# Row maxima 30 steps ahead of their exponentials rather than 32, and a side plan laid out anew

## The chip, the cores and the metric

One core of a Trainium2 chip runs the whole kernel. TensorE (PE in the profile) multiplies, VectorE (DVE), ScalarE (ACT) and GpSimd (POOL) work elementwise, SyncE (SP) issues nearly all DMAs. The metric is the device time of one execution in microseconds; lower is better. Three runs of the kernel before gave 1772.64, 1775.31 and 1781.6 us, median 1775.31.

## The reference

Eight batches of 1024 tokens with 128 channels pass two blocks, each a modulated layer norm, an attention, another norm and a feed-forward part. Cut to what matters:

```python
# block 0: one head of width 32, causal; scores of 0 are masked too
h = layernorm(x)*(1+ca)+sa;  x = x + ga * softmax(mask(QK/sqrt(32))) @ (h @ (Wvdown@Wvup))
h = layernorm(x)*(1+cb)+sb;  e = argmax(h@Wg+bg) % 8;  x = x + gb * relu(h@We[e]+be[e]) * p
# block 1: 16 heads of width 8, full attention over 1024 tokens
h = layernorm(x)*(1+ca)+sa;  weight = softmax(q k^T / sqrt(8));  x = x + ga * ((weight@v)@Wout+bout)
h = layernorm(x)*(1+cb)+sb;  x = x + gb * ((h@W1[b]+b1[b])@W2[b]+b2[b])
```

The 16-head attention is the bulk: 8 x 16 x 1024 x 1024 scores, each of which is computed twice, once for the row maximum and once, transposed, for the exponential.

## The kernel before

**The main line.** Two heads make a pair; there are 64 pairs, eight to a batch. A unit is 128 rows of a pair by 512 columns for both heads, 16 units to a pair, so 1024 units of each kind in all. A maxima unit is two bf16 products on PE (line 792) and one DVE reduction of 128x1024 from PSUM (line 1329). An exponential unit is two products (line 802), which subtract the maxima by way of three extra rows of `q_ops`, and one ACT exponential (line 1028). A values unit multiplies the exponentials with v (eight f32 products, four of them at once; lines 818, 828), and after 16 of them ACT copies the sums out (line 1037) and SP stores them with four DMAs (line 1636).

**Steps.** All five engines walk the same loop over a step number h, from -2*LEAD to 1025. In step h PE issues the exponential products of unit h (if h is at least 0), the maxima products of unit h + 2*LEAD (while there are any), then no, one or two values units (`value_table`, a table worked out beforehand), then the side stages that the plan has put into this step. DVE does the reduction of unit h + 2*LEAD and then its part of the side stages; ACT the exponential of unit h and then its part; POOL and SP have side stages alone. Each engine takes its instructions in this order and waits on semaphores. With LEAD = 16 the first 32 steps (-32 to -1) have maxima alone and the last 32 (992 to 1023) have exponentials alone. Three PSUM buffers go round between the units (`unit_table`), so the exponential products of step h wait for the reduction of step h - 2, and the maxima products of step h for the exponential of step h - 1.

**From maxima to exponentials.** After the last reduction of a pair DVE joins the halves (stage `maxima`), one step later POOL splits the result into three bf16 parts (`nm_split`, lines 1477 to 1480), five steps after that PE transposes them (`nm`), ACT copies, and SP writes them to `q_ops` with two DMAs (line 1612). The exponentials of the pair wait for those.

**Side stages.** Everything else is cut into stages: block 0 and the feature part of block 1 for batch b run beside the attention of batch b-1, the output part (`sums`, `numerators`, `wout_mm`, `stats_b`, `apply_b`, `x_wff`, `channels_b`, `ffn`) of batch b beside the attention of b+1 and its end. `front_line`, `half_line`, WEIGHTS_LINE, BACK_LINE and NM_LINE are lists of (gap in steps, stage); `lay_out` walks them and moves a stage on to the next step that is free. A step is free when no other stage fills the one side bank of PSUM in it (modulo 128, since a batch is 128 steps) and the stage's engine, DVE or ACT, has no other side stage there. `make_plan` repeats the result for each batch, 128 steps apart. Stages before step -2*LEAD run ahead of the loop in the order of the list ALONE. `value_table` then spreads the values units: it minimizes a sum of squared loads of the steps, in which SWITCH is the charge for a kind of product that a step has, and LIGHT is the load below which a step counts as equal.

The stages that the prediction speaks of: `hm` (POOL, line 1462) multiplies the features of 128 tokens with the expert masks, which SP has written to DRAM and fetched back (`masks_out`, `masks_load`, line 1596); it needs the `moe` stage of two tiles before to be done. `moe_a` and `moe` (PE) are the expert products of a tile, which read `hm`. `residual` (POOL, lines 1470, 1471) closes block 0. `stats` and `stats_b` are DVE statistics (1087, 1090) followed by small POOL operations (1357 to 1359); `apply` and `apply_b` (POOL, line 1365) normalize; `channels` (PE, line 608) transposes the result, `qk1` makes q and k, and `parts` (POOL, lines 1414 to 1417) splits them into bf16 parts, which SP stores with three DMAs each (line 519) after waiting for the split. `load_operands` (SP, line 526) fetches a later pair's operands with four DMAs; LOAD_BEFORE sets its step.

Of the kernel before, what the change touches and what calls it, by code (L numbers as in the profile page):

```python
# [41 lines left out]
SLOTS = 4  # L42
VW = DH + 1
COLUMN_TILE = 32
LEAD = 16
PAIRS = B * HEADS // 2
PERIOD = T * HEADS // 2
UNITS = 2 * T
# [7 lines left out]
def chunks(i):  # L56

    return [(c, min(BANK, (i + 1) * P - c)) for c in range(0, (i + 1) * P, BANK)]


def blocks(i):

    some = list(range(1 if i == T - 1 else 0, i + 2))
    return [some[c:c + 4] for c in range(0, len(some), 4)]
# [9 lines left out]
def front_line():  # L74

    out = [(0, ("stats", 0, 0, 0)), (1, ("stats", 0, 0, 1)), (1, ("stats", 0, 1, 0)), (1, ("stats", 0, 1, 1)),
           (0, ("apply", 0, 0)), (1, ("apply", 0, 1)), (3, ("channels", 0, 0)), (1, ("g0", 0)), (1, ("channels", 0, 1)),
           (1, ("g0", 1)), (1, ("v0",)), (0, ("later",)), (1, ("gates",))]
    for n in range(T + 3):
        if 2 <= n < T + 2:  # L80
            out += [(1, ("transpose_p", n - 2, c)) for c in range(len(blocks(n - 2)))]
        if 1 <= n < T + 1:
            out += [(1, ("softmax", n - 1))]
        if n >= 3:
            out += [(0, ("times_v", n - 3))] + ([(2, ("up", n // 7))] if n - 3 in (3, T - 1) else [])
        if 1 <= n < T + 1:
            out += [(1, ("exp0", n - 1))] + ([(0, ("sums0", n // 5))] if n in (4, T) else [])
        if n < T:
            out += [(0, ("scores", n, c)) for c in range(len(chunks(n)))]
    return out  # L90


def half_line(half):

    first = 4 * half
    out = [(0, ("stats", 1, half, 0)), (1, ("stats", 1, half, 1)), (2, ("apply", 1, half)), (3, ("channels", 1, half)),
           (2, ("wg", half)), (1, ("top", half, 0)), (1, ("top", half, 1)), (1, ("index", half, 0)), (1, ("index", half, 1)),
           (0, ("gating", half, 0)), (2, ("onehot", half)), (0, ("gating", half, 1)), (2, ("onehotT", half)), (1, ("over_gating", half)),
           (0, ("masks_out", half)), (3, ("masks_load", half)), (6, ("hm", first)), (2, ("hm", first + 1)), (1, ("moe_a", first))]
    for t in range(first, first + 4):  # L100
        out += [(3, ("moe_a", t))] if t > first else []
        out += [(1, ("moe", t))] + ([(1, ("hm", t + 2))] if t < first + 2 else [])
    out += [(1, ("residual", half)), (2, ("stats", 2, half, 0)), (1, ("stats", 2, half, 1)), (1, ("apply", 2, half)), (3, ("channels", 2, half))]
    for w in range(2):
        out += [(2 - w, ("qk1", w, half)), (0, ("parts", w, half))]
    return out + [(1, ("v1", half))]
# [25 lines left out]
ON_DVE = {"stats", "softmax", "up", "wg", "top", "index", "onehot", "over_gating", "wff", "wout_mm", "stats_b", "ffn", "maxima"}  # L132
ON_ACT = {"exp0", "gating"} | {name for name, by in EMPTIED_BY.items() if by == "act"} - {"nm"}

FRONT_FROM, WEIGHTS_FROM, BACK_FROM, LOAD_BEFORE = -200, 90, 132, 11

SWITCH, LIGHT = 0.9, 5.1


def quarters(*stage):  # L140
# [4 lines left out]
def lay_out():  # L145
# [6 lines left out]
    def put(line, b, h):  # L152
        ending = False
        for gap, stage in line:
            fills, part = stage[0] in EMPTIED_BY, stage[0].endswith("_a")
            h, stage = h + (1 if ending else gap), (stage[0], b, *stage[1:])
            on = "dve" if stage[0] in ON_DVE else "act" if stage[0] in ON_ACT else None
            if not ending and (line is not NM_LINE or fills):
                while (fills or part) and h % batch in filled or part and (h + 1) % batch in filled or on and h % batch in busy[on]:
                    h += 1  # L160
            if fills or part:
                filled.add(h % batch)
            if part:
                filled.add((h + 1) % batch)
            if on:
                busy[on].add(h % batch)
            ending = part
            at[stage] = h
        return h

    for pair in range(HEADS // 2):
        put(NM_LINE, pair, UNITS * (pair + 1) - 2 * LEAD)
    put(WEIGHTS_LINE, 0, WEIGHTS_FROM)
    put(BACK_LINE, 0, BACK_FROM)
    put(front_line(), 0, FRONT_FROM)
    for half in range(HALVES):
        put(half_line(half), 0, at["up", 0, half] + 1)
# [28 lines left out]
def make_plan():  # L206
# [4 lines left out]
    for (name, n, *more), at in lay_out().items():  # L211
        pairs = name in [stage[0] for gap, stage in NM_LINE]
        for b in range(B):
            h, stage = at + 2 * b * PERIOD, (name, b * HEADS // 2 + n if pairs else b, *more)
            if stage in first:
                continue
            if h < -2 * LEAD:
                ahead.append((h, stage))
# [86 lines left out]
def unit_table():  # L305

    order = []
    for h in range(-2 * LEAD, PAIRS * UNITS):
        if h >= 0:
            order.append(("exp", h))  # L310
        if h + 2 * LEAD < PAIRS * UNITS:
            order.append(("max", h + 2 * LEAD))
    return order, {unit: at for at, unit in enumerate(order)}
# [32 lines left out]
def build(nc, ctx, x_in, Wq0, Wk0, Wvdown, Wvup, Wg, bg, We, be, c0, wmod0,  # L346
# [187 lines left out]
    def tensor_program():  # L534
# [303 lines left out]
        for bank, u in before_steps.items():  # L838
            if bank:
                pe.wait_ge(S["side_" + u.by], u.emptied)  # L840
        for h in range(-2 * LEAD, PAIRS * UNITS + 2):
            if 0 <= h < PAIRS * UNITS:
# [888 lines left out]
```

## Time and profile before

| | us |
|---|---|
| median of three runs | 1775.31 |
| profiled execution, its own time | 1772.89 |
| its span in the trace | 1771.6 |
| maxima-only steps -32 to -1 | 124.7 to 174.1 |
| one full batch of 128 steps (batches 1 to 5 of the loop) | 205.7 to 205.9 |
| the last reduction of line 1329 starts | 1714.3 |

The page lists the busy time of each engine, the granted clock of PE and the costliest lines; views of the trace give windows, waits and timelines. A number x8 behind a row says how many instructions are merged in it. "SPq" rows are DMA issues; the bracket at a row's end is idle time and what ended it. Step numbers below count within a batch of 128; the batch looked at closely starts at 789.9 us (absolute step 384), its step 19 at 818.0 and its step 48 at 867.5.

### The profile page before, as it was taken

The page shows a single profiled execution, that of the slowest core. Times are in us where ns is not written, and L with a number is a line of the kernel's source. Part 1 is how long each engine was busy: PE and PEld are TensorE (multiplying, and loading weights), DVE is VectorE, ACT ScalarE, POOL GpSimd, SP SyncE. Part 2 cuts the span into 40 slices and gives each one's busy share as a digit, 9 for nine tenths or more (in the row PEclk, how much of TensorE's full clock was granted, in tenths as well). Part 3 has the DMA queues.
Part 4 walks back from the last instruction along what each step waited for, and adds up shares of the span by engine and source line. Part 5 has one row for each costly group of instructions (what it writes and reads, how often), then busy time and mean ns, then how long its engine had stood idle before and what let it go on. Part 6 is the DMA issues. An engine that isn't in the chain of part 4 may idle for free.

```text
span 1771.6 us, 54921 instructions
## 1 busy us (share of the span) xinstructions
PE 1668.0 (94%) x23327; PEld 658.5 (37%) x23337; DVE 1499.3 (85%) x2257; ACT 1378.6 (78%) x1934; POOL 733.7 (41%) x1195
## 2 busy tenths in 40 slices
PE   5777999999999999999999999999999999999998
PEld 3543433334333343334333343333433343222224
DVE  4669888898889988899888988899888998999973
ACT  4443779887798778887798878987788877887885
POOL 2321345526543465434564365434664355112110
PEclk9998999999999999999999999999999999999999
DMA  2131111122210322112210213103211122201111
GB/s 71 50 122 33 39 56 53 33 63 59 84 59 23 91 71 69 35 37 74 83 56 27 73 48 94 49 24 96 63 59 36 38 73 71 70 24 50 35 28 35
DMA packets 97234, 99.96 MB, mean 56 GB/s; under 512 B 11117, under 2 KB 81437, under 8 KB 96989
## 3 DMA queue, kind: packets, MB, share of 16 engines
q1 hardware_dynamic: 96188, 95.66, 18.1%
q8 instruction: 184, 3.01, 0.7%
q10 hardware_dynamic: 800, 0.79, 0.1%
q14 instruction: 62, 0.50, 0.1%
HBM read 61.02 MB, written 34.57 MB: 54 GB/s over the span
## 4 chain that ended last, share of the span: by engine, by line
PE 67%; DVE 15%; ACT 13%; issue 3%; DMA 1%; POOL 1%; ACTq 0%; SPq 0%; DVEq 0%; POOLq 0%
PE pv_psum L818 23%; PE side_psum L551 15%; PE buffer L802 12%; PE buffer L792 10%; DVE row_max L1329 9%; ACT p L1028 7%; PE side_psum L641 2%; PE side_psum L608 2%; PE buffer L551 1%; ACT o_sb L1037 1%; DVE s L1177 1%; ACT s L946 1%; DVE st_f L1087 1%; ACT s L939 1%; ACT hT_b L1017 1%
## 5 line engine op out<-in xcount | busy, mean ns | idle before, releaser
L1329 DVE TENSOR_REDUCE row_max<-buffer 128x2 f32<-128x1024 f32 x1024 | 1235.3, 1219 | 163.6 <-PE buffer L792 151.0
L1028 ACT ACTIVATE p<-buffer 128x1024 f32<-128x1024 f32 x1024 | 1048.2, 1025 | 209.1 <-PE buffer L802 193.3
L818 PE MATMUL pv_psum<-p,v 128*9 128x256 f32 x8192 | 583.8, 381 | 5.8 <-ACT o_sb L1037 5.2
L792 PE MATMUL buffer<-k_ops,q_ops 48*128 48x512 bf16 x2048 | 396.1, 384 | 17.8 <-ACT p L1028 7.7
L802 PE MATMUL buffer<-q_ops,k_ops 51*128 51x512 bf16 x2048 | 400.5, 388 | 6.7 <-DVE row_max L1329 5.2
L818 PEld LDWEIGHTS pv_psum<-p,v 128*9 128x9 f32 x8192 | 149.7, 89 | 316.8 <-issue 234.0
L802 PEld LDWEIGHTS buffer<-q_ops,k_ops 51*128 51x128 bf16 x2048 | 98.1, 92 | 371.7 <-issue 237.2
L1462 POOL TENSOR_TENSOR hm<-masks,hT_f 128x1024 f32<-128x1024 bf16 x56 | 120.4, 2150 | 107.5 <-PE side_psum L551 107.5
L792 PEld LDWEIGHTS buffer<-k_ops,q_ops 48*128 48x128 bf16 x2048 | 99.4, 94 | 116.5 <-ACT p L1028 98.7
L1477 POOL TENSOR_SCALAR nm_parts<-nm 128x16 bf16<-128x16 f32 x64 | 16.3, 255 | 268.2 <-DVE nm L1254 267.8
L551 PE MATMUL side_psum<-we,hm 128*32 128x128 f32 x3648 | 121.1, 274 | 0.0
L1445 POOL TENSOR_SCALAR rest<-s 128x128 f32<-128x128 f32 (+7 forms) x48 | 102.8, 2142 | 4.2
L551 PEld LDWEIGHTS side_psum<-we,hm 128*32 128x32 f32 x3648 | 95.1, 110 | 21.6 <-issue 19.3
L1439 POOL TENSOR_TENSOR s<-s,consts 128x128 f32<-128x128 f32 x60 | 27.8, 463 | 166.8 <-ACT s L939 166.8
L1357 POOL TENSOR_SCALAR sm_f<-mv_f 128x4 f32<-128x4 f32 x32 | 6.3, 198 | 180.6 <-DVE mv_f L1090 180.0
L551 PE MATMUL side_psum<-hT,g 128*32 128x512 f32 (+3 forms) x624 | 66.0, 494 | 4.2 <-ACT s L939 2.5
L641 PE MATMUL side_psum<-consts,s 128*128 128x128 f32 x281 | 50.9, 297 | 6.1 <-DVE xn_f L1192 4.4
L946 ACT ACTIVATE s<-s,nm 128x1024 f32<-128x1024 f32 (+6 forms) x60 | 51.4, 857 | 6.4 <-DVE nm L1177 5.9
L1365 POOL TENSOR_SCALAR xn_f<-x,sm_f 128x128 f32<-128x128 f32 x112 | 54.0, 497 | 3.8 <-POOL sm_f L1359 3.8
L957 ACT COPY p0T<-side_psum 128x512 f32<-128x512 f32 (+3 forms) x84 | 43.6, 519 | 12.7 <-PE side_psum L641 10.9
L1177 DVE CUSTOM_DVE_ANT_0 s<-s,rest 128x128 f32<-128x128 f32 (+7 forms) x60 | 45.5, 759 | 4.5 <-POOL rest L1445 4.1
L939 ACT COPY s<-side_psum 128x512 f32<-128x512 f32 (+3 forms) x78 | 37.4, 479 | 13.3 <-PE side_psum L551 11.6
(296 smaller groups left out, 1654.8 us busy)
## 6 DMA issues: line engine op xcount, KB each, us to landing
masks<-masks_rows SPq DMA_DIRECT2D x16, 1024.0 KB, 6.5
q_ops<-products SPq DMA_DIRECT2D x128, 96.0 KB
k_ops<-products SPq DMA_DIRECT2D x128, 96.0 KB
products<-q_parts SPq DMA_DIRECT2D x16, 384.0 KB, 2.6
products<-k_parts SPq DMA_DIRECT2D x14, 384.0 KB, 2.8
attention<-o_sb SPq DMA_DIRECT2D x248, 18.0 KB
x<-in_L_attn_inputs SPq DMA_DIRECT2D x8, 512.0 KB, 4.3
products<-q_parts SPq DMA_DIRECT2D x16, 256.0 KB, 3.0
```

The costliest lines, as they stand in the source:

```text
L551: m = e.matmul(out[q:q + COLUMN_TILE, :], weight[:, q:q + COLUMN_TILE], moving, start=start, stop=stop)
L641: m = e.transpose(v[:, j * P:(j + 1) * P], s0_of(b, i)[0][:, k * P:(k + 1) * P], ident)
L792: m = e.matmul(buffer[:, hh, :], q_ops[rows_of(hh, K_MAX), slot, of, i * P:(i + 1) * P], k_ops[rows_of(hh, K_MAX), slot, of, halves(half)[ ...
L802: m = e.matmul(buffer[:, hh, :], k_ops[rows_of(hh, K_EXP), slot, of, kb * P:(kb + 1) * P], q_ops[rows_of(hh, K_EXP), slot, of, halves(half ...
L818: m = e.matmul(pv_psum[q:q + VW, half * QUARTER:(half + 1) * QUARTER], v1[b % 2][:, kb, 2 * hp + hh, :], p_sb[n % KEPT][:, hh, part * QUAR ...
L939: e.copy(s[:, P + at:P + at + w], v[:, 0:w]).then_inc(S["side_act"], 1)
L946: e.activation(s[:, start:P + n], s[:, start:P + n], ACT.Exp, scale=-1.0, bias=nm0[:, i:i + 1], accum_out=acc0[:, i:i + 1]).then_inc(S["p0 ...
L1028: e.activation(p_sb[n % KEPT][:, :, :], unit("exp", n)[0][:, :, :], ACT.Exp).then_inc(S["exp_done"], 1)
L1177: e.tensor_tensor_reduce(out=s[:, P:P + n], in0=s[:, P:P + n], in1=rest[:, 0:n], scale=1.0, scalar=-NEG, op0=ALU.add, op1=ALU.min, accum_o ...
L1329: e.tensor_reduce(mx[pair % 2][:, :, i, half], unit("max", n)[0][:, :, :], axis=AX.X, op=ALU.max).then_inc(S["max_done"], 1)
L1445: e.tensor_scalar(rest[:, 0:n], s[:, P:P + n], 0.0, -NEG, ALU.is_equal, ALU.mult).then_inc(S["masked"], 1)
L1462: e.tensor_tensor(hm[t % 2][:, :, :], masks[:, :, cols], hT_f[:, cols].unsqueeze(1).broadcast_to([C, EXPERTS, P]), op=ALU.mult).then_inc(S ...
```

## The change

LEAD becomes 15: maxima stand 30 steps ahead. The pair's `maxima` stage, and with it `nm_split` and `nm`, come two steps later against the exponentials, so `nm` is 8 steps ahead of the pair's first exponential instead of 10. `load_operands` comes two steps later as well. Since these stages hold steps that others must avoid, the plan comes out otherwise, and five numbers in it are changed too. The stages ahead of the loop stay the same.

```diff
-LEAD = 16
+LEAD = 15
-... (3, ("channels", 0, 0)), (1, ("g0", 0)), (1, ("channels", 0, 1)),
-           (1, ("g0", 1)), ...
+... (3, ("channels", 0, 0)), (2, ("g0", 0)), (1, ("channels", 0, 1)),
+           (0, ("g0", 1)), ...
-        out += [(1, ("moe", t))] + ([(1, ("hm", t + 2))] if t < first + 2 else [])
+        out += [(1, ("moe", t))] + ([(0, ("hm", t + 2))] if t < first + 2 else [])
-FRONT_FROM, WEIGHTS_FROM, BACK_FROM, LOAD_BEFORE = -200, 90, 132, 11
+FRONT_FROM, WEIGHTS_FROM, BACK_FROM, LOAD_BEFORE = -201, 90, 132, 11
-SWITCH, LIGHT = 0.9, 5.1
+SWITCH, LIGHT = 1.2, 5.1
```

Followed through `lay_out` and `value_table`, the steps of a full batch are (before -> after):

| stage | step | stage | step |
|---|---|---|---|
| `onehotT`, second half | 11 -> 15 | `stats_b` (0,0), (0,1), (1,0), (1,1) | 27, 28, 29, 33 -> 27, 28, 29, 32 |
| `masks_load`, second half | 15 -> 19 | `stats` of block 1, first half | 30, 31 -> 25, 30 |
| `moe` of tiles 0 to 3 | 8, 13, 18, 25 -> 10, 14, 18, 22 | `apply_b`, `apply` of block 1 | 31, 32 -> 31, 31 |
| `hm` of tiles 4 to 7 | 21, 23, 29, 34 -> 25, 27, 29, 33 | `channels` of block 1, first half | 35 -> 34 |
| `moe_a`/`moe` of tiles 4, 5 | 27/28, 32/33 -> 28/29, 32/33 | `parts` of q, of k, first half | 37, 40 -> 36, 38 |
| `wout_mm` | 23, 26 -> 23, 26 | `nm` of the pair of step 48 | 38 -> 40 |
| `residual`, first half | 26 -> 23 | `load_operands` | 37 -> 39 |
| values units in steps 0-18, 19-47, 48-127 | 18, 30, 80 -> 19, 31, 78 | values copied and stored | 19, 34 -> 19, 35 |

Both plans have values or tile work in 121 of the 128 steps, and the same side stages. SP's order in a step is `load_operands`, the store of the values, then the plan's stages.

## Rows read from the trace of the kernel before

**Rows 1.** The page: busy us, share of the span, instructions of each engine.
```profile
PE 1668.0 (94%) x23327; PEld 658.5 (37%) x23337; DVE 1499.3 (85%) x2257; ACT 1378.6 (78%) x1934; POOL 733.7 (41%) x1195
```

**Rows 2.** Windows: length, busy us of each engine, granted clock, DMA share, GB/s.
```profile
124.70:174.10 49.40, 38.64 (x320) 15.37 (x322) 46.77 (x81) 13.89 (x33) 6.89 (x19) 0.88 0.15 48
...
789.90:818.00 28.10, 27.81 (x466) 12.38 (x466) 26.30 (x40) 22.99 (x33) 12.45 (x16) 1.00 0.34 99
818.00:867.60 49.60, 48.02 (x822) 21.38 (x822) 41.13 (x59) 36.31 (x44) 31.51 (x41) 1.00 0.21 64
867.60:995.80 128.20, 124.16 (x1595) 44.90 (x1593) 112.96 (x170) 111.06 (x163) 58.68 (x104) 1.00 0.16 49
...
1590.40:1714.30 123.90, 119.27 (x1307) 34.41 (x1308) 118.55 (x123) 102.07 (x110) 17.12 (x43) 1.00 0.14 39
1714.30:1752.00 37.70, 36.49 (x582) 15.66 (x586) 8.00 (x14) 32.88 (x37) 3.64 (x6) 1.00 0.11 29
```

**Rows 3.** Timeline of DVE: start, us, line, operation.
```profile
124.69 4.69 DVE L1329 TENSOR_REDUCE row_max<-buffer 128x2 f32<-128x1024 f32 x4 [0.48 <-PE buffer L792]
...
877.08 1.19 DVE L1329 TENSOR_REDUCE row_max<-buffer 128x2 f32<-128x1024 f32 x1
...
878.87 2.33 DVE L1329 TENSOR_REDUCE row_max<-buffer 128x2 f32<-128x1024 f32 x2
```

**Rows 4.** Timeline of PE, steps 24 to 35; each step begins with line 802.
```profile
825.61 0.39 PE L802 MATMUL buffer<-q_ops,k_ops 51*128 51x512 bf16 x2
...
826.59 0.24 PE L551 MATMUL side_psum<-be,onehotT 128*32 128x128 bf16 x4 [0.37 <-DVE x L1303]
...
827.63 0.39 PE L802 MATMUL buffer<-q_ops,k_ops 51*128 51x512 bf16 x2
...
833.17 0.39 PE L802 MATMUL buffer<-q_ops,k_ops 51*128 51x512 bf16 x2
...
835.13 0.39 PE L802 MATMUL buffer<-q_ops,k_ops 51*128 51x512 bf16 x2
...
836.65 0.39 PE L802 MATMUL buffer<-q_ops,k_ops 51*128 51x512 bf16 x2
...
845.66 0.66 PE L608 MATMUL side_psum<-consts,xn_f 128*128 128x128 f32 x4
```

**Rows 5.** Timeline of POOL, from `hm` of tile 5 to the k split.
```profile
829.37 2.15 POOL L1462 TENSOR_TENSOR hm<-masks,hT_f 128x1024 f32<-128x1024 bf16 x1 [8.38 <-PE side_psum L551]
...
839.48 1.75 POOL L1365 TENSOR_SCALAR xn_b<-x,sm_b 128x128 f32<-128x128 f32 x4
...
843.06 1.75 POOL L1365 TENSOR_SCALAR xn_f<-x,sm_f 128x128 f32<-128x128 f32 x4 [0.18 <-POOL sm_f L1359]
...
851.35 2.35 POOL L1528 TENSOR_TENSOR x<-x,wff 128x1024 f32<-128x1024 f32 x1
...
860.12 1.16 POOL L1417 TENSOR_TENSOR k_parts<-xn_f,k_parts 128x512 bf16<-128x512 f32 x1
```

**Rows 6.** Timeline of SP's DMA issues in the same stretch.
```profile
809.87 0.54 SPq L1596 DMA_DIRECT2D masks<-masks_rows  x1
820.18 3.35 SPq L1636 DMA_DIRECT2D attention<-o_sb  x4
...
848.40 1.47 SPq L526 DMA_DIRECT2D q_ops<-products  x2
...
859.14 1.59 SPq L1612 DMA_DIRECT2D q_ops<-nm_rows  x2
861.31 2.03 SPq L519 DMA_DIRECT2D products<-k_parts  x3
```

**Rows 7.** Tile `masks`: issue to landing of its 16 loads.
```profile
DMA to landing us min/median/max: 5.5/6.5/8.3
```

**Rows 8.** DMA issues by line: a short transfer, KB each, us to landing.
```profile
over_sums_rows<-sums SPq DMA_DIRECT2D x7, 64.0 KB, 1.6
```

More of the change, by code:

```diff
@@ L76, in front_line @@
     out = [(0, ("stats", 0, 0, 0)), (1, ("stats", 0, 0, 1)), (1, ("stats", 0, 1, 0)), (1, ("stats", 0, 1, 1)),
-           (0, ("apply", 0, 0)), (1, ("apply", 0, 1)), (3, ("channels", 0, 0)), (1, ("g0", 0)), (1, ("channels", 0, 1)),
-           (1, ("g0", 1)), (1, ("v0",)), (0, ("later",)), (1, ("gates",))]
+           (0, ("apply", 0, 0)), (1, ("apply", 0, 1)), (3, ("channels", 0, 0)), (2, ("g0", 0)), (1, ("channels", 0, 1)),
+           (0, ("g0", 1)), (1, ("v0",)), (0, ("later",)), (1, ("gates",))]
     for n in range(T + 3):
```

## The prediction
> **What bounds the kernel now.** I read the page first: PE is busy 94% of the span, DVE 85% [rows 1]. Then the windows by stage, since the share is an average [rows 2]. In the 32 steps that have maxima alone DVE is busy 46.8 of 49.4 us: DVE bounds them. In the long middle a batch of 128 steps takes 28.1 + 49.6 + 128.2 = 205.9 us, and PE is busy 27.8 + 48.0 + 124.2 = 200.0 of them; the granted clock is 1.00 there, so PE at its full clock bounds the middle, and what isn't PE's own work are short waits. From 1590 to 1714 DVE is busy 118.6 of 123.9 us and bounds again. The last 37.7 us have exponentials alone, and PE is busy 36.5.
>
> The middle's steps have fixed prices, which the timeline of PE shows [rows 4]. A step with two values units and no side stage goes from 835.13 to 836.65, 1.52 us. One with one values unit and the four-tile stage `moe` goes from 833.17 to 835.13, 1.96. A values unit is half of what a pair of them adds, 0.44; so exponential and maxima products with their changeover take 0.64, and a four-tile stage 0.88 to 0.90. A wait shows as a step above its price: the step from 825.61 to 827.63 has `moe_a` alone (0.64 + 0.90 = 1.54) and took 2.02, because `moe_a` right behind `wout_mm` waits for DVE to empty the one side bank (0.37 idle in its row).
>
> By this rule the number of values units, tile stages and changeovers decides PE's own work, and both plans have the same per batch. What the change can move are the ends and the waits.
>
> **The change part by part.**
>
> *The ends.* Two steps with maxima alone go. Four reductions in a row start at 124.69 and take 4.69 us, and two take 2.33 to 2.36 [rows 3], so one is 1.13 to 1.18; DVE bounds this stretch, its other work stays and now lies in 30 steps: -2 x 1.15 = -2.3 us. At the other end steps 992 and 993 get a reduction that they hadn't. A step there costs 37.7 / 32 = 1.18 on average, and one of the DVE-bound stretch before it 123.9 us over 102 steps (890 to 991) = 1.21, so by these averages nothing is lost; but the lightest of the exponential-only steps have less PE work than a reduction takes (0.39 and less of products beside one values unit [rows 4]); I take +0.25 each, +0.5. Ends: -1.8 us.
>
> *Steps 48 to 127 and 0 to 18.* The table puts 78 values units instead of 80 into the first and 19 instead of 18 into the second: -0.88 and +0.44. The chain of side stages keeps its distances, because it slides as a whole by two steps. In 0 to 18, `moe_a` no longer stands right behind `onehotT`, and the two steps of `top` have two values units each in place of one of them having one, so DVE's four long steps there are better covered: I take back 0.5. In 48 to 127 `wff_a` now follows `transpose_p` without a values unit to cover the emptying by ACT, +0.2. Together -0.1 and -0.7 per batch. Seven passes of the first and six of the second, and a seventh without block 0 at -0.3: -0.7 - 4.5 = -5.2 us. Bounds: each of these waits is between nothing and the 0.48 that the `moe_a` step lost above, so 3 us to either side over the run.
>
> *Steps 19 to 47* (49.6 us before, of which PE idles 1.6). Three things come together here, in the six passes that have the output part (the first pass has none and comes out at +0.3).
> First, `masks_load` goes from step 15 to 19, behind the four stores of values on SP. Those were issued from 820.18 to 823.53, the load at 809.87 [rows 6]. Now it is issued at 823.6 (step 19 at 818.0 in both, so clock times compare). Its landing takes 6.5, 5.5 at least and 8.3 at most [rows 7]: 830.1. POOL's `hm` for tile 4 starts then; before, it ran at 818.8.
> Second, POOL's queue behind it. Two `hm` of 2.15 end at 834.4. The small operations of `stats_b` wait for DVE's statistics. DVE's turn is 1.12 for a reduction and 1.79 with statistics beside it (877.08 to 878.87 [rows 3]); for steps 25 to 30 that makes the statistics of step 28 ready at 835.6. Small operations 1.6, `hm` 2.15, small ones 1.8 (between 841.23 and 843.06 [rows 5]), two normalizations of 1.75: 835.6 + 1.6 + 2.15 + 1.8 + 3.5 = 844.6. `channels` of step 34 needs that. PE comes there with 15 steps x 0.64 + 15 values units x 0.44 + 8 four-tile stages x 0.90 + `nm` 0.15 = 23.5, at 841.6 with 0.1 for the clock, and is at the side stage 1.0 later, 842.6 to 842.7. So PE waits 1.9 us. Before, the normalization ended at 844.81 and `channels` ran at 845.66, a step later: no POOL wait.
> Third, SP. From the normalization to the end of the k split POOL took 861.28 - 844.81 = 16.5 us before [rows 5], and the queue is the same but for its order: 861.1 after. SP comes to `parts` of q (step 36) and of k (38) before `load_operands` (39) and `nm` (40). Before, the k split was the last: the maxima rows went out at 859.14, ahead of the k stores at 861.31 [rows 6]. Now they are queued behind the wait for the k split, the three k stores (2.05), four operand loads (1.47 + 1.43), and one output store of 0.5: 861.1 + 5.45 = 866.6. Two issues of 0.8, the second landing 1.6 after it begins: 869.0. I bound this landing by 1.6 (the shortest seen [rows 8]) and 3.0 or more if the 768 KB of k parts lie before it; I take the short one, since the rows are 6 KB. PE reaches step 48 at 842.7 + 1.9 + the rest of step 34 and the 13 steps 35 to 47 (23.8) = 868.4 and waits 0.6.
> So step 48 starts at 869.0 rather than 867.5: +1.5 us, six times +9.0, and the first pass +0.3: +9.3 us. Bounds: if POOL and SP hold nobody up, the stretch costs its own work plus 0.5 of bank waits, 48.2, which is -1.4 x 6 = -8.4; if masks land at 8.3 and the rows take 3.0, it is 1.8 + 1.4 more, less some of the first that is absorbed, +2.5 x 6 = +15 on top.
>
> The Trainium skill bears on the last point (DMA: Bandwidth & Descriptors, "Queues, rings and completion order"): a semaphore's increment lands only after every earlier write of the same DMA engine, so a small transfer signals no sooner than the large ones issued before it. No row here shows the landing of the maxima rows. By that rule the landing would be at the long end, and the slower case below would be the likely one; the sum doesn't use it.
>
> Sum: -1.8 - 5.2 + 9.3 = +2.3 us on the profiled execution's own 1772.9, so 1775.2. The median of the runs shown lies 2.4 above it: 1777.6, rounded to 1778.
>
> **The rivals.**
> *The maxima rows come later still (slower).* In steps 36 to 48 SP is one queue, and the exponentials of the pair of step 48 wait at its end. From the point where the rows land after 868.4 every microsecond is paid six times. With 8.3 for the masks or 3.0 for the rows, about +2.5 a pass on top, +15: 1793. For: the slack was 867.5 - 861.6 = 5.9 us before and I count it as used up; DVE's statistics, which POOL waits for, stand in six of the steps 25 to 32 without the extra values units that covered them. Against: waits on PE give POOL and SP their time back. Chance 0.24.
> *The chain doesn't bind (faster).* If `hm` of tile 4 starts early enough, or PE arrives at 34 later than I count because DVE's statistics hold it anyway, one wait takes the other's place, and the removed bank waits (0.48 behind `wout_mm`, 0.4 in front of `qk1`) count: 9.3 - (-8.4) = 17.7 less, 1760. For: `residual` and `moe` of tile 3 come three steps earlier, POOL idled 8.38 us before `hm` at 829.37 [rows 5] and has this time to give. Against: that idle time is where the masks are now awaited. Chance 0.21.
> *It does nothing in the middle.* Waits exchanged one for one, only the ends count: 1773.5. It lies inside my forecast's range; chance 0.10.
> My forecast as it stands: 0.45.
>
> **How the numbers follow.** Within 0.5% is about what a measurement of this kernel can tell from no change: 1766.4 to 1784.2. The forecast's own range is 1769 to 1785. It and the third rival put 0.50 inside and leave 0.03 and 0.02 on the slower and faster side. The slower rival reaches from 1783 to 1796 and is 0.23 outside, the faster one from 1758 to 1767 with 0.20 outside. Faster 0.22, same 0.52, slower 0.26. For 8 in 10 the range takes in half of each rival: 1762 to 1790.
>
> **What would show it.** The maxima-only stretch at 47.1 us instead of 49.4. In each of six passes `channels` behind a POOL wait of 1 to 2 us at step 34; SP issuing the maxima rows of the pair of step 48 behind the k stores; `masks` loads of the second half after the four stores. A batch at 205.9 + 1.5 - 0.8 = 206.6 us; 209 would mean the slower rival, 204 the faster. I am wrong in the mechanism if PE's waits in steps 19 to 47 are for DVE or ACT rather than for POOL and the DMA.

## The result

| | before | after |
|---|---|---|
| median of the runs | 1774.31 us (1772.64 to 1781.6, 4 runs) | 1788.46 us (1786.21 to 1790.69, 4 runs) |
| span of the profiled execution | 1771.6 us | 1788.8 us |
| ratio | | 1.0081, 95% interval 1.0061 to 1.0102 |

The change makes the kernel 0.8% slower. The page of the kernel after, engines first, then the one group whose row says where to look (columns as in [rows 1]; in the second line count, busy us, mean ns, idle before and what ended it):

```profile
PE 1667.2 (93%) x23325; PEld 658.4 (37%) x23335; DVE 1497.0 (84%) x2257; ACT 1377.0 (77%) x1934; POOL 732.1 (41%) x1195
...
L802 PE MATMUL buffer<-q_ops,k_ops 51*128 51x512 bf16 x2048 | 400.7, 388 | 22.7 <-DMA q_ops<-nm_rows 13.6
```

No engine works longer than before [rows 1]; the 17 us by which the traces differ are waits. The exponential products of line 802 now wait 13.6 us for a DMA, the maxima rows. The windows of the kernel after that answer to [rows 2] (length, busy us of PE, PEld, DVE, ACT, POOL, granted clock, DMA share, GB/s):

```profile
128.70:176.20 47.50, 36.89 (x312) 14.82 (x316) 43.59 (x75) 13.86 (x33) 5.46 (x16) 0.87 0.10 31
796.60:825.90 29.30, 28.55 (x474) 12.53 (x476) 27.51 (x43) 23.43 (x34) 12.76 (x16) 1.00 0.31 91
825.90:878.20 52.30, 48.17 (x834) 21.45 (x831) 41.30 (x60) 36.32 (x44) 33.89 (x46) 1.00 0.27 81
878.20:1004.60 126.40, 122.78 (x1575) 44.62 (x1575) 111.22 (x165) 110.72 (x163) 55.80 (x97) 1.00 0.14 43
1732.50:1769.30 36.80, 34.77 (x542) 14.76 (x534) 7.26 (x13) 30.27 (x33) 3.62 (x6) 0.95 0.12 30
```

Steps 19 to 47 of this pass (the fourth batch of steps) took 52.3 us instead of 49.6, with PE busy 48.2 and 48.0: the wait grew from 1.6 to 4.1. By the start of line 802, the batch looked at in the kernel before begins at 789.41 us, not at 789.9 as [rows 2] cuts it; so steps 0 to 18 grew from 28.5 to 29.3, and steps 48 to 127 shrank from 127.8 to 126.4. The starts of line 802 in both traces give the whole account. A pass is one batch of 128 steps, numbered from 0; passes 1 to 6 have all the side work (us, after minus before, sums over the passes named):

| stretch | measured | forecast |
|---|---|---|
| start to the first reduction (124.7 -> 128.7) | +4.0 | 0 |
| from there to the first exponential products | -1.3 | -2.3 |
| pass 0 | -2.6 | -0.5 |
| passes 1 to 6, steps 0 to 18 | +4.0 | -0.6 |
| passes 1 to 6, steps 19 to 47 | +16.7 | +9.0 |
| passes 1 to 6, steps 48 to 127 | -5.4 | -3.8 |
| pass 7, and what follows it | +1.8 | +0.5 |
| sum | +17.2 | +2.3 |

Not all of it is the change's. In the first line nothing is altered, and the first reduction started at 124.2, 124.2, 126.0, 126.6, 127.0, 127.3, 127.6, 128.1, 128.4 and 130.8 us in the ten other profiled executions below. Pass 0 scatters as well: it took 204.5 us in the kernel before, and 202.8 in the last experiment, which is the same kernel up to there. Passes 1 to 6 repeat: 1212.0 us together in the kernel before and 1211.8 in that experiment, against 1227.3 in the changed kernel. These 15.3 us are the part of the account that one trace can bear.

The chain that ended last tells the main one in the trace's own words: in this stretch it runs from DVE over POOL and SP to the DMA (start, us, engine, tile, line; PE's steps before it and rows between left out):

```profile
843.01 0.40 DVE st_b L1087 x2
843.43 0.26 DVE mv_b L1090 x2
844.31 1.02 POOL sm_b L1359
845.33 2.12 POOL hm L1462
847.95 1.01 POOL sm_f L1359
...
850.69 1.71 POOL xn_f L1365 x4
...
857.84 2.36 POOL x L1528
...
867.68 1.19 POOL k_parts L1417
868.89 0.36 SPq L519
...
872.79 0.69 SPq L526
873.53 0.45 SPq L1672
874.03 0.79 SPq L1612
874.86 3.18 DMA q_ops<-nm_rows
878.18 0.39 PE buffer L802 x2
```

In the kernel before the same stretch of the chain runs through PE, with single pieces of ACT and DVE of at most 1.1 us between. The two places where PE waits for this chain, in the timeline of PE of the kernel after:

```profile
852.55 0.63 PE L608 MATMUL side_psum<-consts,xn_f 128*128 128x128 f32 x4 [1.43 <-POOL xn_f L1365]
...
874.52 0.39 PE L802 MATMUL buffer<-q_ops,k_ops 51*128 51x512 bf16 x2
...
878.18 0.39 PE L802 MATMUL buffer<-q_ops,k_ops 51*128 51x512 bf16 x2 [2.07 <-DMA q_ops<-nm_rows]
```

Step 34 took 3.14 to 3.15 us in each of the six passes, 1.47 above the 1.68 that it takes where POOL is in time (third experiment). Step 47 took 4.47, 4.00, 3.66, 4.37, 2.70 and 3.16 us, where two values units alone cost 1.52: 13.2 us over.

### The profile page after: what moved, and what is told of

The parts are those of the page before. It is cut to its first block, busy times and chain, and to the rows that moved or that the text cites. A ratio compares the mean times of both kernels' runs of the same rounds, so it can differ in the third digit from the quotient of the medians.

```text
span 1788.8 us, 54924 instructions
## 1 busy us (share of the span) xinstructions
PE 1667.2 (93%) x23325; PEld 658.4 (37%) x23335; DVE 1497.0 (84%) x2257; ACT 1377.0 (77%) x1934; POOL 732.1 (41%) x1195
## 4 chain that ended last, share of the span: by engine, by line
PE 57%; DVE 18%; ACT 10%; POOL 6%; issue 4%; DMA 3%; SPq 2%; ACTq 0%; POOLq 0%; DVEq 0%
PE pv_psum L818 19%; PE side_psum L551 11%; PE buffer L802 11%; DVE row_max L1329 10%; PE buffer L792 9%; ACT p L1028 6%; PE side_psum L641 2%; PE buffer L551 2%; DMA q_ops<-nm_rows 1%; ACT s L946 1%; PE side_psum L608 1%; ACT o_sb L1037 1%; SPq L526 1%; DVE st_f L1087 1%; POOL hm L1462 1%
## 5 line engine op out<-in xcount | busy, mean ns | idle before, releaser
L802 PE MATMUL buffer<-q_ops,k_ops 51*128 51x512 bf16 x2048 | 400.7, 388 | 22.7 <-DMA q_ops<-nm_rows 13.6
L1439 POOL TENSOR_TENSOR s<-s,consts 128x128 f32<-128x128 f32 x60 | 28.5, 475 | 187.7 <-ACT s L939 187.7
L1470 POOL TENSOR_TENSOR xn_f<-xn_f,gates 128x512 f32<-128x512 f32 x14 | 17.9, 1276 | 115.1 <-ACT xn_f L979 115.1
L1365 POOL TENSOR_SCALAR xn_f<-x,sm_f 128x128 f32<-128x128 f32 x112 | 53.5, 491 | 2.7 <-POOL sm_f L1359 2.7
L957 ACT COPY p0T<-side_psum 128x512 f32<-128x512 f32 (+3 forms) x84 | 43.3, 515 | 13.4 <-PE side_psum L641 12.3
```

What stands on the lines that cost most here:

```text
L802: m = e.matmul(buffer[:, hh, :], k_ops[rows_of(hh, K_EXP), slot, of, kb * P:(kb + 1) * P], q_ops[rows_of(hh, K_EXP), slot, of, halves(half ...
L957: e.copy(pT[:, some[0]:some[-1] + 1, :].rearrange("p k q -> p (k q)"), v[:, 0:len(some) * P]).then_inc(S["side_act"], 1)
L1365: m = e.tensor_scalar(xn[:, t, :], src[:, t, :], sm[:, 0, t:t + 1], sm[:, 2, t:t + 1], ALU.add, ALU.mult)
```

## The experiments

Ratios are to the kernel before, measured again beside each group of experiments (medians 1776.04, 1774.93 and 1774.29 us), with their 95% interval.

**The k stores behind the rows.** The first kernel takes the k split and its stores out from ahead of the maxima rows:

```diff
+                if name == "parts" and at[1:] == [1, 0]:
+                    kept.append(at)
-                if name in stages:
+                elif name in stages:
                     stages[name](*at)
+                if name == "nm":
+                    while kept:
+                        parts(*kept.pop())
```

> The changed kernel, but SP issues the k stores of the first half (steps 38) only after the maxima rows of step 40. Theory A, SP's queue: in the changed kernel the step before 48 took 2.70 to 4.47 us in the six full passes where its work is 1.52, in all 13.2 us over, because the rows wait behind the k split, three k stores and four operand loads. Without the k split and its stores ahead they go out about 4 us earlier: about 13 us less than the changed kernel, ratio to before about 1.001. Theory B, the delay has another source that the rows only share (DMA load in that stretch): less than 4 us off the changed kernel, ratio 1.006 or more.

Measured: 1771.33 us, ratio 0.9976 (0.9960 to 0.9992), 17 us less than the changed kernel. Step 47 took 1.52 us in all six passes; step 34 stayed at 3.18. Theory A holds, B falls. Passes 1 to 6 took 1212.9 us, 14.4 less than in the changed kernel: the 13.2 us of the waits and 1.5 of two slow steps behind the longest of them (below), less 0.2 at step 34. The rest lies in the start and the last pass (3.8 us between the two traces).

**Masks first.** SP loads the masks of step 19 ahead of that step's values stores:

```diff
+            for name, *at in plan.get(h, ()):
+                if name == "masks_load":
+                    stages[name](*at)
             if h in copied_at:
                 values_out(copied_at[h])
             for name, *at in plan.get(h, ()):
-                if name in stages:
+                if name in stages and name != "masks_load":
                     stages[name](*at)
```

> The changed kernel, but SP issues masks_load of step 19 ahead of the four stores of values of that step, 3.3 us earlier. If late masks make POOL late (my prediction's first point), the POOL wait at step 34 (1.5 us in six passes) goes or shrinks: 3 to 9 us less. The rival says DVE: POOL's small operations after the two hm waited from 841.9 to 843.8 us for the statistics of step 28, so hm can come 1.9 us earlier and nothing follows: 0 +- 2 us against the changed kernel, step 34 still 3.1 us long.

Measured: 1789.31 us, ratio 1.0078 (1.0051 to 1.0105), the changed kernel's. In the fourth batch the masks were issued 2.7 us ahead of step 19 rather than 5.7 behind its start, so 8.4 us earlier and not 3.3. Step 34 stayed at 3.14 to 3.15 us. The masks are late in the changed kernel, but they are not what the normalization waits for in the end; the rival holds. The timeline of POOL in the changed kernel shows both waits, first the masks, then DVE's statistics (bracket: idle us and releaser):

```profile
837.62 4.26 POOL L1462 TENSOR_TENSOR hm<-masks,hT_f 128x1024 f32<-128x1024 bf16 x2 [2.09 <-DMA masks<-masks_rows]
843.77 0.20 POOL L1357 TENSOR_SCALAR sm_b<-mv_b 128x4 f32<-128x4 f32 x1 [1.89 <-DVE mv_b L1090]
```

With the masks first (the same place in this experiment's timeline) the first wait is gone, and the second has grown by what it gave:

```profile
836.13 4.27 POOL L1462 TENSOR_TENSOR hm<-masks,hT_f 128x1024 f32<-128x1024 bf16 x2
844.42 0.20 POOL L1357 TENSOR_SCALAR sm_b<-mv_b 128x4 f32<-128x4 f32 x1 [4.01 <-DVE mv_b L1090]
```

**The wait at step 34.** POOL does the normalization that `channels` needs before the other one of step 31:

```diff
-            for name, *at in plan.get(h, ()):
+            for name, *at in sorted(plan.get(h, ()), key=lambda stage: stage[0] == "apply_b"):
                 if name in stages:
                     stages[name](*at)
```

> The changed kernel, but POOL does the normalization of block 1 (step 31) before that of the output part, so channels of step 34 can go 1.75 us earlier. Theory A, waits in series: the 1.5 us of step 34 go, and since POOL's sum and SP's queue stay the same, PE reaches step 48 earlier and waits there 1.5 us longer: within 2 us of the changed kernel. Theory C, waits add up independently: about 9 us less.

Measured: 1801.83 us, ratio 1.0151 (1.0123 to 1.0178): 13 us slower than the changed kernel. Neither theory expected that. Step 34 went to 1.68 us, as both said, and step 47 grew to 4.47 to 5.71, as A said: PE came earlier and waited for the same rows. What is new are steps 48 and 49, with a price of 1.58 and 1.55, which took 2.48 to 2.91 and 1.82 to 2.83. The windows of this kernel around the wait of the first full pass (columns as above) and its timeline of PE:

```profile
455.00:459.40 4.40, 0.34 (x10) 0.06 (x4) 0.60 (x1) 0.23 (x1) 0.00 (x0) 1.00 0.58 167
459.40:466.00 6.60, 6.51 (x96) 3.09 (x100) 3.75 (x4) 3.78 (x5) 1.27 (x2) 0.74 0.30 82
466.00:474.00 8.00, 7.83 (x98) 2.31 (x96) 7.86 (x19) 6.08 (x8) 4.79 (x11) 1.00 0.09 17
```
```profile
459.37 0.39 PE L802 MATMUL buffer<-q_ops,k_ops 51*128 51x512 bf16 x2 [4.06 <-DMA q_ops<-nm_rows]
461.85 0.61 PE L802 MATMUL buffer<-q_ops,k_ops 51*128 51x512 bf16 x2
```

PE had 0.34 us of work in 4.4 us, then the granted clock fell from 1.00 to 0.74 over the next 6.6 us, that is, part of it went at the lower level of 1.2 GHz; the products of 0.39 us took 0.61. So a long wait on PE can be paid a second time: here steps 48 and 49 took 1.5 to 2.6 us too much in each of the six passes, 12.3 in all. In the changed kernel it happened in one pass of six, with steps 48 and 49 at 2.51 and 2.13 us behind the 4.47:

```profile
455.00:459.00 4.00, 2.44 (x36) 0.70 (x28) 2.43 (x2) 1.87 (x2) 0.00 (x0) 1.00 0.48 155
459.00:463.00 4.00, 2.68 (x42) 1.68 (x44) 1.23 (x1) 1.02 (x1) 0.00 (x0) 0.72 0.37 102
```

**Both edits.** The diffs of the first and the third experiment together, nothing else.

> Both of the edits of the first and third kernel. Theory A: with the rows out of the way behind step 48, the 1.5 us of step 34 are now really saved: 13 + 9 = 22 us less than the changed kernel, so some 8 us faster than before (ratio 0.995). Theory B: as in the first kernel, under 4 us, or the 9 us of the norms alone.

Measured: 1763.01 us, ratio 0.9931 (0.9907 to 0.9955), 25 us less than the changed kernel, where 22 were expected, and 8 less than with the first edit alone. The same swap that cost 13 us with the rows late saves 8 once they are in time: the waits are in series. Four passes have a step 47 of 1.52 us, two still wait (2.21 and 2.61).

**The lead alone.** In the kernel before, all else as there:

```diff
-LEAD = 16
+LEAD = 15
```

> The kernel before with LEAD = 15 alone; its plan comes out with channels at step 38, the first half's parts at 42 and 44, behind the maxima rows of step 40 on SP. Theory A: the rows aren't held up, no long step 47; the middle costs about what it cost before, the ends give their 1 to 2 us: ratio 0.997 to 1.002. If the lead itself were the cost (8 steps from nm to the first exponential too few), it would stay at 1.006 or more.

Measured: 1808.44 us, ratio 1.0200 (1.0176 to 1.0225). My expectation (at most 1.002) was wrong by some 30 us, and in the place: no pass waits for the rows, but step 38 takes 4.79 to 5.25 us, since `channels` there finds POOL even later (`PE side_psum L608 <- POOL xn_f L1365: 19.9, 13, 3.1` in its list of waits: us in all, times, longest). Steps 39 and 40 behind it take 2.8 and 2.2 to 2.3; in the fourth batch the granted clock was 0.51 from 860.40 to 867.40 us; PE had waited 3.07 us up to 861.87. It fell so at this step in all six passes. The plan that comes out of the old numbers with the new lead is worse than the one of the changed kernel; the new numbers repair more than half of it, and not all. So neither half of the change by itself makes the wait at step 47.

**The plan alone.** In the changed kernel:

```diff
-LEAD = 15
+LEAD = 16
```

> The changed kernel with LEAD = 16 again, all other numbers new: the side plan then has the parts at steps 31 and 32, ahead of the maxima rows of step 38 with the operand loads of 37 between. Theory A: six or seven steps lie between the parts and the rows, more than POOL's backlog of about 5, so no wait at 48: ratio 0.995 to 1.004.

Measured: 1773.95 us, ratio 0.9994 (0.9984 to 1.0005). As expected; steps 19 to 47 take 48.6 us in each of passes 1 to 6, and passes 1 to 6 together 1211.8, as in the kernel before.

**The table of values.**

```diff
-SWITCH, LIGHT = 1.2, 5.1
+SWITCH, LIGHT = 0.9, 5.1
```

> The changed kernel with SWITCH = 0.9: the same side plan, only the table of values units differs. Both theories: the queue on SP is the same, so the long step 47 stays and the kernel stays within 4 us of the changed one, ratio 1.006 to 1.010.

Measured: 1784.34 us, ratio 1.0065 (1.0040 to 1.0090); step 34 at 3.14, step 47 at 2.78 to 4.46, and passes 1 to 6 together 1226.7. Where the values units stand is not the cause.

**The operand loads behind the rows.**

```diff
-... BACK_FROM, LOAD_BEFORE = -201, 90, 132, 11
+... BACK_FROM, LOAD_BEFORE = -201, 90, 132, 9
```

> The changed kernel with LOAD_BEFORE = 9: the four operand loads come at step 41, behind the maxima rows. The rows are issued 2.9 us earlier, still behind the k stores. If the rows' landing (3.3 us after the second issue in the changed kernel) is set by their place in SP's queue alone, the wait before 48 falls by 2.9 us or to nothing in each pass: 11 to 13 us less, ratio about 1.001. If the 768 KB of k stores ahead hold them up, half of it stays: 5 to 8 us less.

Measured: 1773.90 us, ratio 1.0002 (0.9988 to 1.0015), 14.6 us less than the changed kernel. All six steps 47 are 1.52 us. So either of the two things ahead of the rows may go, and the wait goes; it takes both. It isn't free, though: the loads, which come late now, are waited for themselves (1.35 us before the maxima products of step 50 in pass 1), and passes 1 to 6 took 1216.9 us, 4.0 more than with the first edit.

**Both edits, and the loads four steps earlier.**

In the kernel with both edits:

```diff
-... BACK_FROM, LOAD_BEFORE = -201, 90, 132, 11
+... BACK_FROM, LOAD_BEFORE = -201, 90, 132, 15
```

> The kernel with both edits (k stores behind the maxima rows, block 1's normalization first), and LOAD_BEFORE = 15, so that the four operand loads come at step 35, ahead of the q stores' wait, and not between it and the rows. In the kernel with both edits two of six passes still had a long step 47 (2.21 and 2.61 us), where the rows landed 3.2 us after their second issue. Theory A: the rows go out up to 2.9 us earlier and both waits go: 0 to 2 us less than that kernel's 1763, ratio to before 0.992 to 0.994.

Measured: 1763.95 us, ratio 0.9944 (0.9926 to 0.9962). The last two waits are gone, and each of passes 1 to 6 takes 48.67 us from step 19 to 48. In the traces these passes are 1.8 us shorter together (1203.7 against 1205.5), and what comes before them 3.1 us longer, so the time as a whole can't tell the two kernels apart (their intervals overlap). These two are the fastest versions, 0.6 to 0.7% under the kernel before. This trace also closes the account of the changed kernel: its 1203.7 us with no wait at either step, 13.2 for step 47, 8.8 for step 34 and 1.5 for the lower clock give 1227.2, where 1227.3 were measured.

**The rows late in the kernel before.**

```diff
+                if name == "nm" and (h - 38) % (2 * PERIOD) == 0 and 38 < h < 896:
+                    kept.append(at)
-                if name in stages:
+                elif name in stages:
                     stages[name](*at)
+                if name == "parts" and at[1:] == [1, 0] and kept:
+                    nm_stage(*kept.pop())
```

> The kernel before (LEAD = 16), but SP issues the maxima rows of step 38 only after the k stores of step 40, in passes 1 to 6. That makes them 4.2 us later than before: second issue at 864.2 + where PE comes to step 48 at 867.5. With the landing of 3.2 us that the changed kernel showed they land at 867.4, so just in time: 0 to 3 us slower than before (ratio 1.000 to 1.002). With the 1.6 us that my prediction took there would be 1.7 us of slack left and no pass would wait. If being behind the k stores were itself the cost of the changed kernel, and not the 3 us of operand loads and the two steps less of lead on top, this kernel would lose the same 13 us.

Measured: 1773.66 us, ratio 0.9995 (0.9984 to 1.0007). The rows' second issue comes 2.64 to 3.77 us before step 48 instead of 7.34 to 7.51, and no step 47 is longer than 1.52. Standing behind the k stores is harmless by itself. The low end, 2.64, also shows that the rows can land in less than 3.2 us.

**The landing, from the traces above.** The traces keep the single DMA packets, and the 48 packets of 256 bytes behind the two issues of line 1612 are the rows (6 KB each). From the second issue to the last of these packets, in passes 1 to 6:

| ahead of the rows in SP's queue | kernels | us |
|---|---|---|
| k stores; last operand load 12 us before or more | eighth and last experiment | 1.49 to 1.52 |
| no k stores; last operand load 8 us before or more | before, lead alone, ninth | 1.49 to 1.52 |
| operand loads, the last 0.7 to 1.9 us before | changed, and all others | 1.53 to 3.07 |

In the changed kernel the last packet came after 2.62, 3.03, 2.68, 2.71, 1.78 and 1.71 us, and PE went on 0.55 to 0.65 later. All k stores had landed there before the rows' second issue. So it is the operand loads that hold up the rows, and not the k stores; in the kernel with both edits, where the k stores stand behind the rows, the rows of the two waiting passes took 3.2 us all the same. Nor is it the output store between the loads and the rows (873.53 us in the chain above): in the eighth experiment it stands directly ahead of the rows too.

## Why the prediction was right and where it was too small

The time fell into the stated range, near its upper end, 10 us above the number forecast; "within 0.5%" had the largest chance and did not come true. That the range held is owed to its width, since it took in half of either rival: the sum itself said +2.3 us, and the medians differ by 14.2. What came true is the slower rival, by its own mechanism and place. Of the 15 us that it put on top of the forecast, the median shows 10.5, and the stretch it speaks of 7.7 (16.7 - 9.0). Passes 1 to 5 took 208.4 us on average (206.9 to 210.2), where I had named 209 for the slower rival.

*The ends* (-1.8). The maxima-only stretch fell from 48.8 to 47.5 us up to the first exponential products, 1.3 instead of 2.3. It differs between traces: 44.4 to 48.2 us (46.5 on average) in the nine with the lead of 30 steps, 48.4 to 50.0 (49.0) in the three with 32, so the 2.3 fits these averages. Pass 7, for which I had +0.5, took 2.9 us more. Its last pair waits for its rows as well (0.82 us in the timeline of PE), since they now stand behind `sums_load` on SP. Another 1.5 us are two steps at the lower clock, 6 us behind that wait; they aren't the change's, since the last experiment, whose last pass is that of the kernel before, has the same two steps as long (2.30 and 1.42 us where the kernel before had 1.31 and 0.94).

*Steps 0 to 18 and 48 to 127.* The second was right in its direction, -5.4 for -3.8 in the six passes. The first was wrong: I took 0.5 back for the better cover of `top`, and the stretch grew by 0.65 a pass, which is the one values unit of 0.44 more and another 0.2. PE's idle time in it went from 0.3 to 0.7 us. Most of that is one wait for DVE's reduction, which stood before step 127 of the kernel before (0.47) and stands before step 1 now (0.47), so that the second stretch lost what the first gained. Together the two came to -0.6 in a pass, where I had -0.8.

*Steps 19 to 47, POOL.* The steps of the forecast against the trace, from the start of step 19 on (818.0 in the forecast's clock, 825.9 in the trace):

| | forecast | measured |
|---|---|---|
| masks issued | 5.6 | 5.7 |
| `hm` of tiles 4 and 5 done | 16.4 | 16.0 |
| small operations of `stats_b` start | 17.6 | 17.9 |
| normalization for `channels` done | 26.6 | 26.5 |
| k split done | 43.1 | 43.0 |
| first issue of the maxima rows | 48.6 | 48.1 |
| PE would reach step 48 | 50.4 | 50.1 |
| rows landed, step 48 starts | 51.0 | 52.3 |

All but the last agree within 0.5 us, the wait at step 34 with 1.47 for 1.9. So the chain, its order and its place were right; that late masks start it was not: the second experiment issued them 8.4 us earlier, and step 34 did not move. DVE's statistics, the second entry in that sum, bind alone.

*Steps 19 to 47, the landing.* This is the term that was mis-sized. I took 1.6 us from the second issue to the landing, by the shortest row [rows 8], "since the rows are 6 KB". It was 2.3 to 3.7 us in the six passes (3.18 in the chain above), and with it the wait before step 48 is 1.2 to 2.9 us instead of 0.6; 13.2 - 3.6 = 9.6 us over six passes. Less the 2.6 by which I had put the wait at step 34 too high (six times 0.43), that is most of the 7.7 us by which the stretch missed its forecast. My long bound of 3.0 was the better value, though not for the reason that I gave, the k parts ahead of the rows. What was missing in the term is the four operand loads directly ahead: without them the last packet of the rows came 1.5 us after the second issue, with them 1.7 to 3.0. Even with nothing ahead 1.6 was short: 1.5 and the 0.6 that PE went on later make about 2.1 (an estimate from these rows; no wait shows it).

The Trainium skill's rule on ordered semaphore writes (DMA: Bandwidth & Descriptors, "Queues, rings and completion order") says that a semaphore's increment lands only after every earlier write of the same DMA engine. I had read more from it, that a small transfer signals no sooner than the large ones ahead. The traces don't show that as the cause: the k stores had landed before the second issue, and it was the rows' own packets that came late, the last of them at 877.55 us in the fourth batch, 2.7 after the second issue and 0.6 before PE went on.

*Not in any case of the forecast:* that a long wait can be followed by a stretch of PE at the lower clock and so be paid again. It cost the changed kernel 1.5 us in one pass behind step 47, and 1.5 to 2.6 in every pass of the third experiment.

What stays open: why the same loads hold up the rows by 0.2 us in one pass and by 1.5 in another, and why the clock falls behind some waits and not behind others.

## What to carry to other kernels

When a plan is shifted, write down for every wait that has slack which queue its producer stands in and what else that queue does between; here the maxima rows, whose second issue had come 7.5 us ahead of step 48, lost that lead to neighbours, of which either alone did no harm. A chain over several engines whose waits lie in series gives nothing for its first wait as long as the last one stands, and can even lose by it; take away the last one first. For the landing of a small transfer take its own packets, and ask what stands directly ahead of it in its queue, rather than take the shortest row of another one.

## What the runs showed of the hardware that was not expected

Behind a wait of PE of 2.88 us in the changed kernel and of 4.06 in the third experiment the granted clock of the next stretch was 0.72 and 0.74, so partly at 1.2 GHz, and steps of 1.55 to 1.58 us took up to 2.91. It did not follow every wait of that size: a wait of 2.78 us in the changed kernel (a step 47 of 4.37) and one of 3.12 in the second experiment have a step 48 of 1.58 behind them. And it came without one: in the last experiment the clock was 0.50 from 1734.90 to 1738.30 us, where the waits of PE in the 15 us before were at most 0.38.

Transfers of 6 KB were held up by 384 KB of loads directly ahead of them in SP's queue (last packet 1.53 to 3.07 us after the issue), and not by 768 KB of stores in the same place (1.49 to 1.52).

And DVE's reductions back to back with a statistics stage took 1.79 us from start to start, where the durations of its five instructions add up to 2.1: consecutive rows overlap, so spacing from start to start is what to add up.
